# The inverse of a head's softmax sums, moved from VectorE to POOL

## The reference

```python
xn = layernorm(x)
q, k, v = split(xn @ w_qkv.T)                  # rope is applied to q and k
scores = einsum('blhd,bmhd->bhlm', q, k) * Dh ** -0.5
attn = softmax(scores)                          # over m, 2048 keys
s = einsum('bhlm,bmhd->blhd', attn, v).reshape(B, L, D) @ w_out.T
onehot = one_hot(argmax(xn @ gate_w.T))         # one expert per token
f = einsum('etd,edh->th', square(relu(xn @ wg)) * (xn @ wu) * onehot, wd)
return x + s * silu(f)
```

## Time and profile before

| what | us |
|---|---|
| median of 3 runs | 1486.63 (1484.91 to 1490.43) |
| profiled execution | 1485.04 |
| its span, first to last instruction | 1483.3 |
| PE busy | 1450.7 (98%) |
| DVE busy | 1346.4 (91%) |
| ACT busy | 1192.4 (80%) |
| POOL busy | 162.1 (11%) |
| reciprocals of `spread` on DVE (L885) | 32, 7.9 together, 246 ns each |

### The profile page before, as it was taken

The page is one execution under the profiler, slowest core; times in us unless marked ns, Lnnn a source line. Parts: engine busy times, 40 slices in busy tenths (PEclk is TensorE's granted clock), DMA queues, the critical chain, the costliest instruction groups (busy, mean ns, idle before and its releaser), DMA issues.

```text
span 1483.3 us, 31996 instructions
## 1 busy us (share of the span) xinstructions
PE 1450.7 (98%) x11197; PEld 652.2 (44%) x11197; DVE 1346.4 (91%) x1979; ACT 1192.4 (80%) x2381; POOL 162.1 (11%) x221
## 2 busy tenths in 40 slices
PE   7999999999999999999999999999999999999988
PEld 5555444434475433343434344434444444434326
DVE  6689999999846999999999999999999999999906
ACT  3653588888867888888888888888888888888890
POOL 5433322200001222000010000000010000000110
PEclk9999999999999999999999999999999999999999
DMA  5875244436263455333332342333323433333323
GB/s 186 277 204 137 65 84 83 76 46 125 39 188 90 80 111 99 52 48 48 48 44 41 48 99 42 46 46 48 48 44 45 97 48 41 48 48 48 69 70 117
DMA packets 79801, 119.55 MB, mean 81 GB/s; under 512 B 28962, under 2 KB 66210, under 8 KB 72738
## 3 DMA queue, kind: packets, MB, share of 16 engines
q1 hardware_dynamic: 73714, 105.82, 36.0%
q0 software_dynamic: 3072, 8.39, 2.2%
q10 hardware_dynamic: 2896, 3.62, 0.7%
HBM read 77.15 MB, written 39.71 MB: 79 GB/s over the span
## 4 chain that ended last, share of the span: by engine, by line
PE 94%; ACT 3%; DVE 1%; issue 1%; DMA 1%; SPq 0%; POOL 0%; ACTq 0%; POOLq 0%
PE ps L1243 39%; PE ps L1257 36%; PE ps L1231 5%; PE ps L1159 3%; ACT arena L658 2%; PE ps L1437 2%; PE ps L1160 1%; PE ps L1390 1%; PE ps L1374 1%; PE ps L1192 1%; PE ps L1184 1%; PE ps L1171 1%; PE ps L1341 1%; ACT x_sb L658 1%; PE ps L1136 0%
## 5 line engine op out<-in xcount | busy, mean ns | idle before, releaser
L1231 PE MATMUL ps<-ks,qs 48*128 48x512 f32 x1984 | 692.7, 444 | 0.0
L1243 PE MATMUL ps<-qs,ks 50*128 50x512 f32 x2048 | 680.6, 435 | 9.3 <-ACT x_sb L658 7.6
L809 DVE TENSOR_REDUCE arena<-ps 128x1 f32<-128x512 f32 x992 | 639.0, 681 | 16.5 <-PE ps L1231 16.2
L658 ACT ACTIVATE arena<-ps 128x512 f32<-128x512 f32 x1056 | 564.3, 605 | 86.9 <-PE ps L1243 79.7
L812 DVE TENSOR_REDUCE arena<-ps 128x1 f32<-128x1024 f32 x496 | 603.7, 1217 | 0.8 <-PE ps L1231 0.7
L658 ACT ACTIVATE x_sb<-ps 128x512 f32<-128x512 f32 x992 | 535.3, 598 | 64.9 <-PE ps L1243 44.9
L1243 PEld LDWEIGHTS ps<-qs,ks 50*128 50x128 f32 x2048 | 329.5, 184 | 485.0 <-issue 200.9
L1231 PEld LDWEIGHTS ps<-ks,qs 48*128 48x128 f32 x1984 | 325.2, 184 | 16.5 <-DVE arena L809 9.3
L1257 PE MATMUL ps<-arena 128*32 128x256 f32 (+1 forms) x3104 | 308.5, 469 | 5.5 <-ACT arena L658 4.1
L1257 PE MATMUL ps<-x_sb,arena 128*32 128x256 f32 (+1 forms) x2960 | 290.2, 464 | 0.0
L1257 PEld LDWEIGHTS ps<-arena 128*32 128x32 f32 x3104 | 62.3, 108 | 125.6 <-issue 125.6
(11 more groups left out here) (116 smaller groups left out, 623.2 us busy)
## 6 DMA issues: line engine op xcount, KB each, us to landing
qs<-parts_d SPq DMA_DIRECT2D x186, 128.0 KB
ks<-parts_d SPq DMA_DIRECT2D x186, 128.0 KB
parts_d<-arena SPq DMA_DIRECT2D x64, 256.0 KB, 2.8
xs_d<-arena SPq DMA_DIRECT2D x13, 384.0 KB, 3.5
arena<-xs_d SPq DMA_DIRECT2D x13, 384.0 KB, 3.8
ys_d<-arena SPq DMA_DIRECT2D x13, 384.0 KB, 2.8
x_sb<-in_x SPq DMA_DIRECT2D x2, 2048.0 KB, 13.1
onum_d<-arena SPq DMA_DIRECT2D x124, 32.0 KB
```

The costliest lines, as they stand in the source:

```text
L658: nc.scalar.activation(prob_of(pi, s, kb)[:, c * W:(c + 1) * W], ps[:, bank, :], ACT.Exp, scale=SCALE).then_inc(exp_done[bank], 1)
L809: nc.vector.tensor_reduce(most[head_slot][:, tile, u:u + 1], ps[:, AB + lo, :], AX.X, ALU.max).then_inc(a_reduced[u], 1)
L1231: ins = nc.tensor.matmul(ps[:, AB + c, :], qs[head_slot][ABASE:ABASE + KR, tile * P:(tile + 1) * P].bitcast(F32R), ks[head_slot][ABASE:ABA ...
L1243: nc.tensor.matmul(ps[:, bank, :], ks[s][at:at + KS, kb * P:(kb + 1) * P].bitcast(F32R), qs[s][at:at + KS, c * W:(c + 1) * W].bitcast(F32R ...
```

## The change

VectorE's reciprocal is taken out, and with it the memset of `spread[1]` and the odd count. POOL makes the inverse as a tensor_tensor power of the tile with a column of minus ones (`minus_one`), right behind the `stage` of the same slot: `invert(s, n)` inverts the sums of pair n - 1. Behind `stage(0, 3, 1, 3)` it waits for the sums of head 5. SP's order is not touched; `store_inverse` waits for POOL.

```diff
+        minus_one = sb("minus_one", [P, 1])
             def store_inverse(head, s, pi):
-                sp.wait_ge(rec_ready[s], pi + 1 + s)
+                sp.wait_ge(rec_ready[s], pi + 1)
-            nc.vector.memset(spread[1], 1.0)
-            def invert(s, n):
-                dve.wait_ge(spread_in[s], past(n * 16))
-                nc.vector.reciprocal(spread[s], spread[s]).then_inc(rec_ready[s], 1)
             def step(pi, last_pair, s, kb):
-                if kb == 5:
-                    invert(1 - s, pi + s)
+            nc.gpsimd.memset(minus_one[:], -1.0)
+            def invert(s, n):
+                pool.wait_ge(spread_in[s], past(n * 16))
+                TT(spread[s], spread[s], minus_one[:].to_broadcast([P, L // P]), ALU.pow).then_inc(rec_ready[s], 1)
             scatter(0, SC)
             stage(0, 1, 0, 1)
+            invert(0, 1)
             scatter(SC, 2 * SC)
             stage(0, 1, 1, 1)
+            invert(1, 1)
             scatter(2 * SC, NT)
             pool.wait_ge(v_staged[1], 2)
+            for s in range(2):
+                pool.wait_ge(rec_ready[s], 1)
...
             for pi in range(2, FB):
                 for s in range(2):
                     stage(0, pi, s, pi)
+                    invert(s, pi)
             for s in range(2):
                 stage(0, FB, s, FB)
+                invert(s, FB)
             collect(0, SC)
             stage(0, FB + 1, 0, FB + 1)
+            invert(0, FB + 1)
             collect(SC, 2 * SC)
             stage(0, FB + 1, 1, FB + 1)
+            invert(1, FB + 1)
             collect(2 * SC, NT)
             for m in range(1, NC):
                 ...
                         stage(b, j, s, j + b * (H // 2))
+                        invert(s, j + b * (H // 2))
                 weigh(m - 1)
+            invert(0, NP)
```

## The result

The changed kernel takes 1503.74 us (median of four, 1502.82 to 1506.49), the kernel before 1485.77 beside it: 1.0123 times as long, 95% interval 1.0101 to 1.0145, 18 us slower. I had forecast 1488.5, "no change", with 1500 as the upper end. The profiled execution took 1506.49 us, its span is 1504.7.

The account below looks back on a forecast made before the run. The prediction took VectorE's reductions to pace the steady part. Its sum was -4.8 us for reciprocals, +8.7 for a PE stop at head 8, -1.2 for a hidden pause: +2.7 us, forecast 1488.5 us, range 1485 to 1493.

Parts of the forecast that it names:

- The pace is VectorE's: Steady heads: VectorE, busy 37.87 of 38.00 us, sets the pace, and PE runs at it with short stalls.
- 31 reciprocals at 0.155 us, 4.8 us: VectorE, heads 0 to 30: each reciprocal removed gives back 0.155 us, 4.8 us in all.
- the prediction's list of signs: What would show it: steady heads 0.16 us shorter, head 7's store near 565, one PE stop of 8 to 9 us.
- Rival 3: Steady heads: VectorE's time isn't given back, only the stop at head 8 counts: +7.0 us, about 1493; chance 0.07.
- `invert(1, 4)` behind 28 gathers: POOL, inverse of head 7: late, with the chunk load behind it; PE stops 8.7 us at head 8's last step.
- `invert(1, 3)` and `invert(0, 4)`: POOL around the gathers: the first makes them 0.2 us later, the second is covered by a 1.61 us wait.
- The power at 0.5 us: POOL: each power of 128x16 takes 0.5 us, twice the nearest row, with bounds of 0.2 and 4.6 us.
- rival 2: POOL: the power is dear; at 2.7 us the time is 1494, at 4.6 us 1500; chance 0.18.
- The drain of 11.4 to 13.6 us: Chunk load ahead of head 9's shift: its second transfer drains 11.4 to 13.6 us after issue, ending at 578.2 to 580.4.
- The shift waits for the bulk ahead of it: Transfer queue at head 9: the shift's four small transfers land with the chunk's drain, 0.9 us more, PE on at 580.2.
- Rival 1: Head 9's shift isn't held up by the chunk load: stop about 1 us, gain -4.3 us, some 1482; chance 0.13.
- the pause of the earlier trace: PE at head 8's last step in the kernel before: a pause of 1.22 us, taken as hidden in the new stop.

Follow-up runs that it names:

- e8: The kernel before without VectorE's reciprocals and with nothing on POOL instead, the inverse left out: 1479.62 us, 0.9956 times the kernel before.
- e9: The kernel before with two more reciprocals of a 128x16 spare tile ahead of each one on VectorE: 1490.87 us, 1.0044 times the kernel before.
- e1: The changed kernel with POOL's stage and inverse of head 7 after 20 gathers, not after 28: 1479.19 us, 0.9969 times the kernel before.
- e2: The changed kernel with each power replaced by a product with minus one, same place and waits: 1500.53 us, 1.0107 times the kernel before.
- e5: The kernel before, first chunk load held until head 9's maxima, head 11's six loads held until head 9's shift landed: 1497.28 us, 1.0079.
- e3: The changed kernel with the first chunk load put behind head 9's shift and the load after it: 1485.60 us, 1.0009 times the kernel before.
- e4: The kernel before with the first chunk load held until head 9's maxima are ready, right before its shift: 1505.79 us, 1.0139.
- e6: The kernel before with only the first chunk's 1 MB of values held until head 9's maxima are ready: 1489.96 us, 1.0037.
- e7: The kernel before with only the first chunk's 1 MB of broadcast inverses held until head 9's maxima are ready: 1500.52 us, 1.0102.

## Why the prediction was wrong

The mechanism was the one that was forecast: one late inverse, the chunk load right behind it, the shift behind that, one stop of PE. What failed were sizes in its sum, which gave +2.7 us: the price of the power, the length of the drain and the gain on VectorE, and a term was missing.

- *The pace is VectorE's*: right (e8, e9).
- *31 reciprocals at 0.155 us, 4.8 us*: the size was off; 0.083 a head, 2.6 us. I read 0.16 us from its start to the next start and didn't look at the next pair of reductions, 1.23 us already in the earlier trace rows; others take 1.28, and 0.16 less what comes back there is the net price. So steady heads shrank by half of the 0.16 us in the prediction's list of signs; nor do these rows show its 37.90 us as the length of a head, which was 38.23 before. Rival 3 (nothing given back) is wrong.
- *`invert(1, 4)` behind 28 gathers is the one that costs*: right; PE has its one stop there, and e1, which moves this one alone, removes it. The powers at `invert(1, 3)` and `invert(0, 4)` stop nothing by themselves, but they make the gathers, and so this one, later.
- *The power at 0.5 us*: failed, 2.90 us (31 of 31, 2.89 to 2.95, the first among them), within the bounds (0.2 and 4.6) and not near the row I chose. By the gathers it stood three times in the chain, as the prediction wrote: the store came at 572.7 and not at 564.9, 7.8 us. With a product of 0.21 us it came at 563.8 (e2). So rival 2, which had a chance of 0.18, was the likelier side on the price; its formula gave +6 us for 2.9 us, some 1495, a third of the loss, and 1.7 of the 7.8 us are over it.
- *The drain of 11.4 to 13.6 us*: failed. From the broadcast's issue to PE it took 21.1 us where the sum had 13.4: 7.7 us. Both rows it came from were without the six loads that SP issues right behind the shift; with these held it was 15.6 (e5). The 2.2 us from there to 13.4 are not explained.
- *The shift waits for the bulk ahead of it*: right (e3, e4), and more for the broadcast than for the values (e6, e7). Rival 1 is wrong.
- *Not in the sum at all*: PE's clock after the stop, 0.50 until 600. For the first work behind the stop (595.35 to 600.37) it took 5.0 us in the chain where the kernel before took 2.95 (574.10 to 577.05): 2.1 us.

The sum with what was measured: stop 8.7 + 7.8 + 7.7 = 24.2, and 0.9 as PE got there at 570.56 and not at 571.5, less 0.4 as the second chunk transfer followed the store by 1.50 us: 24.7, measured 24.79. Then -2.6 + 24.8 + 2.1 - 1.2 = +23.1 us. Between the two profiles it is 21.4 us of span; about 2 us stand between heads 5 and 6, where the kernel before ran part of 455 to 470 at the lower clock and the changed one did not:

```profile
455.00:470.00 15.00, 15.00 (x83) 6.62 (x82) 8.63 (x12) 11.18 (x21) 1.96 (x2) 0.89 0.65 122
```

```profile
455.00:470.00 15.00, 15.00 (x101) 6.92 (x102) 10.13 (x14) 13.18 (x25) 4.82 (x3) 1.00 0.60 101
```

Open: this stretch and the pause of the earlier trace rows are what e1 and e8 are faster by beyond 2.6 us, in their profiles. All five profiles without the reciprocal have 1.00 from 460 to 470; of the six with it four have 0.83 there and two (e4, e6) have 1.00. e9 has that stretch and not the pause. So neither follows from the reciprocal alone; whether they are chance, or the reciprocal makes them likelier, wasn't settled. The medians say 18.0 us for the change, 3 less than the profiles: the profiled run of the changed kernel was the slowest of its four.

## What to carry to other kernels

When a producer is moved to an engine with an in-order queue of its own, look for the one place where that queue is behind, and then for what the consumer's queue has to do next: a bulk transfer that slips to a place in front of a small urgent one can hold it for most of its drain, here 3.7 us for 1 MB of plain rows and 14.8 us for a broadcast of 1 MB. A drain is to be priced with what will be issued behind it, and the price of an unknown operation, where it stands several times in one chain, from the far bound. A small operation on the pace-setting engine is to be priced at the start of the instruction after the next one, not at the next start: here half of the 0.16 us came back.

## What the runs showed that I had not expected

- A power of 128x16 on POOL takes 2.90 us, a product of the same form 0.21.
- A broadcast of 1 MB ahead of four 4 KB transfers stopped PE for 14.8 us, 1 MB of plain rows for 3.3 us.
- After stops of 24.8, 18.95 (e4) and 16.5 us (e2) PE ran at 0.50 for another 5, 13 and 12 us, so a shorter stop need not give back its whole difference. Why it was 5 in one and 13 in another stays open.
